# Scaling the message weights and making their low half on GpSimd, with the taps' sums behind the fifth turn

## The chip, the cores and the metric

One core of one Trainium2 chip runs the whole program. The metric is the device time of one execution in microseconds (us), lower is better. The engines are named as in the profile: PE is TensorE's matmul, DVE is VectorE, ACT is ScalarE, POOL is GpSimd, and SP is the engine that issues nearly all transfers.

## The reference

64 graphs of 256 nodes with 256 features go through two layers, each behind a layer norm, a ReLU and a residual sum. The first layer is a graph convolution. The second has a convolution branch (a 1-wide one, conv1, with a batch norm, and then a 17-wide one, conv2, with another), a message branch, and a GRU that joins both.

```python
h = relu(layernorm(x));  x = x + relu(norm_adj @ h @ W.T + b)        # layer 0
h = relu(layernorm(x))                                              # layer 1 on h
c = relu(bn1(conv1(h)));  c = bn2(conv2(c));  x_conv = relu(c + h)
s = h @ w_se.T + b_se;    A = exp(-dist(s, s))
msg = relu(h @ w_msg.T + b_msg);  x_nmp = A @ msg
x = x + gru([x_conv, x_nmp], h)
```

bn1's scale g / sqrt(v + eps) is multiplied into conv1's weights, and bn2's into the 17 taps of conv2.

## The kernel before

The program is written by hand for each engine, with explicit semaphores. An engine executes its own list in order, and a wait_ge holds everything behind it on that engine. There are three stages: the first takes the 64 batches one after the other, the second multiplies spectra, the third runs the GRU. The change touches only the start of the first.

The first stage is a software pipeline of turns. In turn i each engine calls its function first_tensor, first_vector, first_scalar, first_gpsimd or first_sync with i, and each of them does a step for batch i, another for batch i - 1, and so on: statistics of batch i, hd (the normalised input) for i - 1, the aggregation agg (L618) for i - 2, out0 (matmuls with w0, the first matmuls of a turn on PE) for i - 3, the second norm xn for i - 4, transposes (L666) for i - 4, and for i - 5 the products of the second layer. So turn 5 is the first in which batch 0 reaches the second layer: xn is transposed, copied to xt by ACT (L411), split into a high half xxh (ACT, L342) and a low half xxl (DVE, L442), and multiplied on PE with wse (into SXN, 6 matmuls of 256 columns) and then with w1m (into CM1 and CM0, 12 matmuls of 512 columns). In turn 6 DVE adds the bias to CM0 (tcm, L433), and makes uv (L451), which PE's distance product (L627) waits for.

All matmuls of this kind take each operand as a high and a low half, and three products of halves make one product. So each weight has to be split once before its first use: high = copy (ACT), low = weight - high (DVE before the change). For w1m there is a step ahead of that: conv1's half of the raw weights st_w1 is multiplied with the row s1r of bn1's scales (L1388), which ACT copies out of PSUM (L1303, semaphore normrow). w1m has two halves side by side for each input block, conv1's weights and the messages' weights, 128x1024 in all. The change's short description speaks of the messages' weights; the instructions scale columns 0 to 255 of each block, and make the low half of all 1024 columns.

For the taps DVE multiplies bn2's scales into a table and sums it (s2m L1397, s2t L1400, semaphore s2t). The taps themselves are scaled on POOL from turn 10 on.

Before turn 5 ACT, DVE and POOL each wait for clo >= 3 (the low halves of w0, w1m and wse exist) and s2t >= 2 (the taps' sums exist). I call this the barrier. Some buffers of turn 5 and later lie over the staging buffers (st_w1, s2m and their neighbours). PE waits for normrow >= 2 before turn 5 and for clo >= 3 ahead of its first product with wse.

SP's list, with the loads of later batches, hangs on DVE's statistics (semaphores st0 and deg0).

Of the kernel before, what the change touches and what calls it, by code (L numbers as in the profile page):

```python
# [11 lines left out]
ALU = mybir.AluOpType  # L12
# [103 lines left out]
half one ident_in col_in eye2_in w0_in b0_in tt_in w1_in se_in bm_in ft_in gt_in tap0 tap1 s2t  # L116
consts crs diag rows normrow w1s chi clo ones taps
ldx0 ldx1 lda0 lda1 lat0 lat1 st0 ag0a ag0 deg0 degm rs0 dd sd sbias hd ah agg aghi aglo
# [8 lines left out]
def gnn_kernel(nc, x, adj, adjt, w0t, w1mt, wset, wgt, w2r, bc, cols, ftab, gtab, ttab, eye, out):  # L127
# [19 lines left out]
    with ExitStack() as ctx:  # L147
        S = {n: ctx.enter_context(nc.semaphore(n)) for n in NAMES}
# [13 lines left out]
        taps = keep("taps", [119, NW, 256])  # L162
# [88 lines left out]
        TURNS = NB + 11  # L251
# [331 lines left out]
        def first_tensor(e, i):  # L583
# [46 lines left out]
            if live(i, 5):  # L630
                b = i - 5
                e.wait_ge(S["xxhi"], b + 1)
                e.wait_ge(S["xxlo"], b + 1)
                e.wait_ge(S["clo"], 3)
                multiply(e.e, mm3([{c: h[:, c, :] for c in range(2)} for h in wse],
                                  [{c: h[:, c * 256:c * 256 + 256] for c in range(2)} for h in xx],
                                  P[SXN][:, 0:256], True, True, [(0, 0), (1, 1)])).then_inc(S["s"], 1)
# [12 lines left out]
            if live(i, 5):  # L650
                b = i - 5
                for k, n, name, freed in ((CM1, 1, "cm1", "tcm1"), (CM0, 0, "cm0", "tcm0")):
                    e.wait_ge(S[freed], b)
                    multiply(e.e, mm3([{c: h[:, c * 256 + n * 128:c * 256 + n * 128 + 128] for c in range(2)}
                                       for h in xx],
                                      [{c: h[:, c, :] for c in range(2)} for h in w1m],
                                      P[k][:, :], True, True, [(0, 0), (1, 1)])).then_inc(S[name], 1)
# [631 lines left out]
        def _(scalar):  # L1289
# [23 lines left out]

            e.wait_ge(S["clo"], 3)
            e.wait_ge(S["s2t"], 2)
            for i in range(5, TURNS):
                first_scalar(e, i)
# [49 lines left out]
        def _(vector):  # L1367
# [16 lines left out]
            first_vector(e, 3)  # L1384
            e.wait_ge(S["normrow"], 1)
            e.wait_ge(S["w1_in"], 16)
            for k in range(2):
                t = vector.tensor_tensor(st_w1[:, k, 0:256], st_w1[:, k, 0:256], s1r[:, :], ALU.mult)  # L1388
            t.then_inc(S["w1s"], 1)
            first_vector(e, 4)  # L1390
            e.wait_ge(S["chi"], 2)
            vector.tensor_tensor(w1m[1][:, :, :], st_w1[:, :, :], w1m[0][:, :, :], ALU.subtract).then_inc(S["clo"], 1)
            e.wait_ge(S["chi"], 3)
            vector.tensor_tensor(wse[1][:, :, :], st_se[:, :, :], wse[0][:, :, :], ALU.subtract).then_inc(S["clo"], 1)
            e.wait_ge(S["normrow"], 2)
            e.wait_ge(S["tt_in"], 16)
# [3 lines left out]
            vector.tensor_reduce(s2t[:, :], s2m[:, :, :], AX_X, ALU.add).then_inc(S["s2t"], 1)  # L1400
            e.wait_ge(S["clo"], 3)
            e.wait_ge(S["s2t"], 2)
            for i in range(5, TURNS):
                first_vector(e, i)
# [37 lines left out]
        def _(gpsimd):  # L1442
# [13 lines left out]
            gpsimd.tensor_tensor(cold[:, 0:4], cold[:, 20:24], half[:, 0:4], ALU.pow).then_inc(S["crs"], 1)  # L1456
            for i in range(2, 5):
                first_gpsimd(e, i)
            e.wait_ge(S["clo"], 3)
            e.wait_ge(S["s2t"], 2)  # L1460
            for i in range(5, TURNS):
                first_gpsimd(e, i)
# [100 lines left out]
```

## Time and profile before

| what | us |
|---|---|
| median of 3 runs | 1773.26 (1773.23 to 1773.27) |
| the profiled execution's own time | 1773.39 |
| its span (first to last instruction) | 1771.6 |

A row of a timeline has the start in us from the span's beginning, the duration, the engine, the line of the kernel, the operation, its output and inputs, and their shapes.
### The profile page before, as it was taken

What the parts mean: (1) busy time and instruction counts of PE and PEld (TensorE: products, weight loads), DVE (VectorE), ACT (ScalarE), POOL (GpSimd) and SP (SyncE); (2) the same over time, 40 slices, a digit from 0 to 9 for tenths busy, and PEclk for the clock granted to TensorE, in tenths of its full rate; (3) what the DMA queues carried; (4) which work ended last, traced back from release to release, by engine and by line L of the source; (5) the groups of instructions that cost most, each with busy time, mean ns of one, the idle gap of its engine ahead of it and who ended that gap; (6) DMA issues with size and microseconds to landing.
All of it is one profiled execution on the core that took longest, in us unless ns stands there. A gap on an engine that the chain in (4) does not pass through costs nothing.

```text
span 1771.6 us, 30896 instructions
## 1 busy us (share of the span) xinstructions
PE 1757.3 (99%) x10778; PEld 1556.6 (88%) x10778; DVE 1201.1 (68%) x2318; ACT 999.2 (56%) x1787; POOL 817.7 (46%) x988
## 2 busy tenths in 40 slices
PE   8999999999999999999999999999999999999998
PEld 7999999999999999999988888888888888888887
DVE  8999999999999956655664544544545545545445
ACT  6888888888888866666642333332333333333322
POOL 5788888888777637655731221221221212212211
PEclk9999999999999999999999999999999999999999
DMA  6567666666666454444674345445345353454442
GB/s 223 174 201 214 203 211 205 211 204 200 197 192 202 147 167 156 168 166 166 238 213 105 71 105 123 97 107 113 74 112 122 88 119 82 98 120 99 104 96 42
DMA packets 531865, 262.70 MB, mean 148 GB/s; under 512 B 366215, under 2 KB 494471, under 8 KB 531710
## 3 DMA queue, kind: packets, MB, share of 16 engines
q1 hardware_dynamic: 531166, 260.66, 53.5%
q8 instruction: 87, 1.43, 0.4%
q14 instruction: 68, 0.56, 0.1%
q10 hardware_dynamic: 544, 0.07, 0.0%
HBM read 151.58 MB, written 109.05 MB: 147 GB/s over the span
## 4 chain that ended last, share of the span: by engine, by line
PE 96%; issue 1%; DVE 1%; POOL 1%; DMA 1%; ACT 0%; SPq 0%; POOLq 0%; ACTq 0%; DVEq 0%
PE P L111 73%; PE P L618 6%; PE P L1025 4%; PE P L877 4%; PE P L647 4%; PE P L709 4%; PE P L666 2%; PE P L627 1%; DMA at<-in_adjt 0%; POOL axl L581 0%; DMA eye<-in_eye 0%; POOL af L578 0%; DVE sm L489 0%; DVE sm L495 0%; DVE xct L1039 0%
## 5 line engine op out<-in xcount | busy, mean ns | idle before, releaser
L1004 POOL TENSOR_TENSOR xnx1l<-xnf,xnx1h 128x1024 fp32r<-128x1024 f32 x16 | 44.3, 2771 | 393.2 <-ACT xnx1h L997 393.2
L1004 POOL TENSOR_TENSOR xnx0l<-xnf,xnx0h 128x1024 fp32r<-128x1024 f32 x15 | 40.9, 2729 | 272.9 <-ACT xnx0h L997 272.9
L1130 ACT ACTIVATE nn<-gn,col 128x512 f32<-128x512 f32 x64 | 46.4, 725 | 193.4 <-DVE gn L1151 193.4
L1127 ACT ACTIVATE tr<-P,cold 128x512 f32<-128x512 f32 x64 | 44.2, 690 | 179.8 <-PE P L111 179.8
L1147 DVE SCALAR_TENSOR_TENSOR gn<-tr,gn 128x512 f32<-128x512 f32 x64 | 45.2, 706 | 137.3 <-ACT tr L1127 137.3
L578 POOL TENSOR_TENSOR af<-af,at 128x512 f32<-128x512 f32 x64 | 111.9, 1748 | 40.8 <-ACT af L369 39.7
L581 POOL TENSOR_TENSOR axl<-af,axh 128x512 fp32r<-128x512 f32 x64 | 102.8, 1606 | 54.0 <-ACT axh L387 54.0
L618 PE MATMUL P<-ah,hd 128*128 128x256 f32 x512 | 121.9, 381 | 0.0
L1160 DVE SCALAR_TENSOR_TENSOR tz<-tz,tr 128x512 f32<-128x512 f32 x63 | 43.6, 692 | 109.3 <-ACT tz L1141 109.2
L1141 ACT ACTIVATE tz<-P,cold 128x512 f32<-128x512 f32 x63 | 43.4, 689 | 123.2 <-PE P L111 123.2
L111 PE MATMUL P<-w1mh,xxh 128*128 128x512 f32 x256 | 106.5, 416 | 0.0
L618 PEld LDWEIGHTS P<-ah,hd 128*128 128x128 f32 x512 | 93.3, 191 | 10.3
L111 PE MATMUL P<-w1mh,xxl 128*128 128x512 f32 x256 | 100.5, 393 | 0.0
L111 PE MATMUL P<-w1ml,xxh 128*128 128x512 f32 x256 | 100.2, 391 | 0.0
L501 DVE SCALAR_TENSOR_TENSOR x<-x,x 128x512 f32<-128x512 f32 x64 | 99.8, 1559 | 0.1
L902 DVE TENSOR_TENSOR yo<-P,mt 128x512 f32<-128x512 f32 x78 | 53.5, 686 | 65.4 <-PE P L111 65.4
L1151 DVE TENSOR_TENSOR gn<-gn,P 128x512 f32<-128x512 f32 x64 | 44.0, 687 | 65.2 <-PE P L111 64.6
L1039 DVE SCALAR_TENSOR_TENSOR xct<-P,cold,xnf 128x256 f32<-128x256 f32 x128 | 55.7, 477 | 44.9 <-PE P L1025 44.9
L111 PE MATMUL P<-w0h,agh 128*128 128x256 f32 x256 | 76.9, 301 | 4.9 <-DVE w0l L466 2.1
L709 PE MATMUL P<-tt_w,taps 119*128 119x140 f32 (+1 forms) x592 | 80.8, 282 | 0.0
L729 ACT COPY wf<-P 128x420 f32<-128x420 f32 (+1 forms) x94 | 46.8, 512 | 59.5 <-PE P L709 59.3
L1025 PEld LDWEIGHTS P<-gt,yt 64*128 64x128 f32 x1280 | 75.2, 187 | 5.6 <-issue 5.6
(214 smaller groups left out, 6401.3 us busy)
## 6 DMA issues: line engine op xcount, KB each, us to landing
xh_d<-xst SPq DMA_DIRECT2D x64, 320.0 KB, 4.9
y_d<-yo SPq DMA_DIRECT2D x80, 256.0 KB, 2.1
yt<-y_d SPq DMA_DIRECT2D x128, 160.0 KB, 4.5
xl<-xh_d SPq DMA_DIRECT2D x36, 512.0 KB, 4.5
x<-in_x SPq DMA_DIRECT2D x64, 256.0 KB, 2.7
a<-in_adj SPq DMA_DIRECT2D x64, 256.0 KB, 3.0
at<-in_adjt SPq DMA_DIRECT2D x64, 256.0 KB, 4.2
x_d<-x SPq DMA_DIRECT2D x64, 256.0 KB, 4.4
```

The source lines that it names most:

```text
L111: done = e.matmul(o, l, r, start=start, stop=stop, skip_group_check=True)
L501: e.e.scalar_tensor_tensor(out=o[:, :, :], in0=o[:, :, :], scalar=0.0, in1=xs[b % 5][:, :, :], op0=ALU.max, op1=ALU.add).then_inc(S["x2"], 1)
L578: e.e.tensor_tensor(af[:, :], af[:, :], at[b % 7][:, :], ALU.mult).then_inc(S["am"], 1)
L581: e.e.tensor_tensor(ax[1][:, :], af[:, :], ax[0][:, :], ALU.subtract).then_inc(S["axlo"], 1)
L618: t = e.e.matmul(P[AG][:, f * 256:f * 256 + 256], hd[b % 2][:, m, f * 128:f * 128 + 128], ah[b % 2][:, m * 256:m * 256 + 256], start=m == ...
L647: t = e.e.matmul(P[k][:, n * 2 * NT:n * 2 * NT + 2 * NT], h1[b % 2][:, n, c * 128:c * 128 + 128], ft[:, :], start=True, stop=True, skip_gr ...
L709: t = e.e.matmul(P[k][:, m * 140:m * 140 + 140], taps[0:n_rows, j0 + m, c * 128:c * 128 + 128], tt_w[0:n_rows, part * 140:part * 140 + 140 ...
L877: t = e.e.matmul(common(chunk)[:, 0:256], xsum[f % 3][:, c, 128 * chunk:128 * chunk + 128], wsum[f % 3][:, c, :], start=c == 0, stop=c == ...
L902: e.e.tensor_tensor(yo[n % 4][:, :].rearrange("p (q o) -> p q o", q=2), main(chunk)[:, :].rearrange("p (q o) -> p q o", q=2), mt[chunk][:, ...
L1004: e.e.tensor_tensor(o[1][:, :, :], xnf[p % 2][:, :, :, :].rearrange("p c i t -> p c (i t)"), o[0][:, :, :], ALU.subtract).then_inc(done, 1)
L1025: t = e.e.matmul(P[idft_bank(b, o)][:, at + first:at + end], y[rows, q, :], gt[rows, g:g + end - first], start=q == 0, stop=q == 4, skip_g ...
L1039: d = e.e.scalar_tensor_tensor(out=t[:, c, :], in0=P[idft_bank(b, c)][:, at:at + 256], scalar=b2[:, c:c + 1], in1=xnf[p % 2][:, c, n, :], ...
```

## The change

- DVE no longer multiplies st_w1 with s1r (two 128x256) and no longer makes w1m's low half (128x1024). POOL does the first between turns 3 and 4 and the second behind turn 5, and signals the second with a semaphore of its own, wlp. PE waits for wlp ahead of the products with w1m in turn 5.
- DVE makes the taps' sums behind turn 5, not ahead of it.
- The barrier of ACT, DVE and POOL stands behind turn 5, and asks for clo >= 2, since w1m's low half no longer counts there. PE's wait ahead of the wse product is clo >= 2 too.

```diff
--- before.py
+++ after.py
@@ -114,7 +114,7 @@
 
 NAMES = """
 half one ident_in col_in eye2_in w0_in b0_in tt_in w1_in se_in bm_in ft_in gt_in tap0 tap1 s2t
-consts crs diag rows normrow w1s chi clo ones taps
+consts crs diag rows normrow w1s chi clo wlp ones taps
 ldx0 ldx1 lda0 lda1 lat0 lat1 st0 ag0a ag0 deg0 degm rs0 dd sd sbias hd ah agg aghi aglo
 out0 u x2 sx20 sx21 st1 ag1a ag1 rs1 n1b xn xnt xt sxt xxhi xxlo s uvf uvh uv cm0 cm1 tcm0 tcm1 h1 mshi mslo
 dist af am axhi axlo nmp nm snm dft0 dft1 xe0 xe1 sxa0 sxa1 sxb0 sxb1
@@ -631,7 +631,7 @@
                 b = i - 5
                 e.wait_ge(S["xxhi"], b + 1)
                 e.wait_ge(S["xxlo"], b + 1)
-                e.wait_ge(S["clo"], 3)
+                e.wait_ge(S["clo"], 2)
                 multiply(e.e, mm3([{c: h[:, c, :] for c in range(2)} for h in wse],
                                   [{c: h[:, c * 256:c * 256 + 256] for c in range(2)} for h in xx],
                                   P[SXN][:, 0:256], True, True, [(0, 0), (1, 1)])).then_inc(S["s"], 1)
@@ -649,6 +649,7 @@
                     t.then_inc(S[f"dft{c}"], 1)
             if live(i, 5):
                 b = i - 5
+                e.wait_ge(S["wlp"], 1)
                 for k, n, name, freed in ((CM1, 1, "cm1", "tcm1"), (CM0, 0, "cm0", "tcm0")):
                     e.wait_ge(S[freed], b)
                     multiply(e.e, mm3([{c: h[:, c * 256 + n * 128:c * 256 + n * 128 + 128] for c in range(2)}
@@ -1311,9 +1312,10 @@
             scalar.copy(s2r[:, 256:7 * NW], P[CM0][:, 0:7 * NW - 256]).then_inc(S["normrow"], 1)
             first_scalar(e, 4)
 
-            e.wait_ge(S["clo"], 3)
+            first_scalar(e, 5)
+            e.wait_ge(S["clo"], 2)
             e.wait_ge(S["s2t"], 2)
-            for i in range(5, TURNS):
+            for i in range(6, TURNS):
                 first_scalar(e, i)
             for n in range(EARLY, UNITS):
                 if n == UNITS - 6:
@@ -1382,25 +1384,19 @@
             vector.tensor_scalar(cold[:, 8:12], cold[:, 8:12], 0.5, None, ALU.mult)
             vector.tensor_scalar(cold[:, 12:14], col[:, 26:28], 0.5, None, ALU.mult)
             first_vector(e, 3)
-            e.wait_ge(S["normrow"], 1)
-            e.wait_ge(S["w1_in"], 16)
-            for k in range(2):
-                t = vector.tensor_tensor(st_w1[:, k, 0:256], st_w1[:, k, 0:256], s1r[:, :], ALU.mult)
-            t.then_inc(S["w1s"], 1)
             first_vector(e, 4)
-            e.wait_ge(S["chi"], 2)
-            vector.tensor_tensor(w1m[1][:, :, :], st_w1[:, :, :], w1m[0][:, :, :], ALU.subtract).then_inc(S["clo"], 1)
             e.wait_ge(S["chi"], 3)
             vector.tensor_tensor(wse[1][:, :, :], st_se[:, :, :], wse[0][:, :, :], ALU.subtract).then_inc(S["clo"], 1)
+            first_vector(e, 5)
             e.wait_ge(S["normrow"], 2)
             e.wait_ge(S["tt_in"], 16)
             vector.tensor_tensor(s2m[:, :, :], s2r[0:119, :].rearrange("p (j o) -> p j o", o=7),
                                  tt_w[:, 560:567].unsqueeze(1).broadcast_to((119, NW, 7)), ALU.mult).then_inc(S["s2t"], 1)
             e.wait_ge(S["s2t"], 1)
             vector.tensor_reduce(s2t[:, :], s2m[:, :, :], AX_X, ALU.add).then_inc(S["s2t"], 1)
-            e.wait_ge(S["clo"], 3)
+            e.wait_ge(S["clo"], 2)
             e.wait_ge(S["s2t"], 2)
-            for i in range(5, TURNS):
+            for i in range(6, TURNS):
                 first_vector(e, i)
             first_stage_done(e)
             weights_lo(e, 0)
@@ -1454,11 +1450,20 @@
             first_gpsimd(e, 1)
             e.wait_ge(S["consts"], 1)
             gpsimd.tensor_tensor(cold[:, 0:4], cold[:, 20:24], half[:, 0:4], ALU.pow).then_inc(S["crs"], 1)
-            for i in range(2, 5):
+            for i in range(2, 4):
                 first_gpsimd(e, i)
-            e.wait_ge(S["clo"], 3)
+            e.wait_ge(S["normrow"], 1)
+            e.wait_ge(S["w1_in"], 16)
+            for k in range(2):
+                t = gpsimd.tensor_tensor(st_w1[:, k, 0:256], st_w1[:, k, 0:256], s1r[:, :], ALU.mult)
+            t.then_inc(S["w1s"], 1)
+            for i in range(4, 6):
+                first_gpsimd(e, i)
+            e.wait_ge(S["chi"], 2)
+            gpsimd.tensor_tensor(w1m[1][:, :, :], st_w1[:, :, :], w1m[0][:, :, :], ALU.subtract).then_inc(S["wlp"], 1)
+            e.wait_ge(S["clo"], 2)
             e.wait_ge(S["s2t"], 2)
-            for i in range(5, TURNS):
+            for i in range(6, TURNS):
                 first_gpsimd(e, i)
             first_stage_done(e)
             for f in range(NF):
```

How the lists stand now, in the place that counts. On DVE, between turn 4 (it ends with L417) and turn 5 (it begins with L442):

```order
 L417 BN_AGGR sm_90<-sm_90 128x2 x2
 L417 BN_AGGR sm_87<-sm_87 128x2 x2
-L1392 TENSOR_TENSOR w1ml<-st_w_118,w1mh 128x1024
-L1394 TENSOR_TENSOR wsel<-st_se,wseh 128x256
-L1397 TENSOR_TENSOR s2m<-s2r,tt_w 119x259
-L1400 TENSOR_REDUCE s2t<-s2m 119x37
+L1389 TENSOR_TENSOR wsel<-st_se,wseh 128x256
 L442 TENSOR_TENSOR xxl<-P,xxh 128x512
 L461 TENSOR_TENSOR ah_73<-at_111,eye_106 128x512
```

Of four instructions one is left there. On DVE again, between turn 5 (it ends with L535) and turn 6 (it begins with L433):

```order
 L417 BN_AGGR sm_88<-sm_88 128x2 x2
 L535 TENSOR_TENSOR tcm<-P,b1m 128x512
+L1393 TENSOR_TENSOR s2m<-s2r,tt_w 119x259
+L1396 TENSOR_REDUCE s2t<-s2m 119x37
 L433 TENSOR_TENSOR tcm<-P,b1m 128x512
 L442 TENSOR_TENSOR xxl<-P,xxh 128x512
```

The two instructions of the taps' sums came here. On POOL, between turn 5 (it ends with L566 of batch 4, which ACT's hd waits for) and turn 6:

```order
 L564 TENSOR_TENSOR sm_90<-sm_90 128x2
 L566 TENSOR_TENSOR sm_90<-sm_90 128x2
+L1463 TENSOR_TENSOR w1ml<-st_w_118,w1mh 128x1024
 L540 TENSOR_TENSOR sm_88<-guard,sm_88 128x2
 L541 TENSOR_TENSOR sm_88<-guard,sm_88 128x2
```

w1m's low half is made behind all ten small instructions of turn 5.

## Rows read from the trace of the kernel before

**Rows 1.** The page's first part: busy us, share of the span, instructions of each engine.
```profile
PE 1757.3 (99%) x10778; PEld 1556.6 (88%) x10778; DVE 1201.1 (68%) x2318; ACT 999.2 (56%) x1787; POOL 817.7 (46%) x988
```

**Rows 2.** Busy us by window, 100 us of the first stage: stretch, PE, PEld, DVE, ACT, POOL, PEclk, DMA.
```profile
100.00:200.00 100.00, 100.00 (x654) 92.18 (x653) 97.73 (x238) 88.45 (x176) 82.09 (x131) 1.00 0.67 206
```

**Rows 3.** Timeline of PE, turns 3 to 7: start, us, engine, line, operation.
```profile
13.10 0.36 PE L111 MATMUL P<-w0h,agh 128*128 128x256 f32 x1 [2.09 <-DVE w0l L466]
...
21.02 1.89 PE L618 MATMUL P<-ah,hd 128*128 128x256 f32 x8
23.77 0.66 PE L666 MATMUL P<-ident,xn 128*128 128x128 f32 x4 [0.86 <-ACT xn L357]
25.26 0.36 PE L111 MATMUL P<-w0h,agh 128*128 128x256 f32 x1 [0.83 <-DVE agl L423]
...
27.39 2.86 PE L618 MATMUL P<-ah,hd 128*128 128x256 f32 x8
29.99 0.37 PE L111 MATMUL P<-xxh,wseh 128*128 128x256 f32 x1
...
30.79 0.40 PE L111 MATMUL P<-w1mh,xxh 128*128 128x512 f32 x1
...
37.89 0.51 PE L627 MATMUL P<-uv 96*128 96x256 f32 x2 [0.53 <-DVE uv L451]
...
42.52 0.36 PE L111 MATMUL P<-w0h,agh 128*128 128x256 f32 x1 [0.25 <-issue]
```

**Rows 4.** Busy us by window, three single microseconds around the clock's fall.
```profile
23.00:24.00 1.00, 0.23 (x2) 0.23 (x3) 1.00 (x3) 1.00 (x3) 0.92 (x2) 1.00 0.63 172
...
26.00:27.00 1.00, 1.00 (x7) 1.00 (x7) 1.00 (x2) 0.47 (x1) 0.00 (x0) 0.50 1.06 371
...
29.00:30.00 1.00, 1.00 (x6) 0.74 (x4) 0.80 (x2) 0.14 (x2) 0.92 (x3) 0.82 0.94 319
```

**Rows 5.** Timeline of DVE, turns 4 to 6.
```profile
20.29 0.72 DVE L1388 TENSOR_TENSOR st_w<-st_w,s1r 128x256 f32<-128x256 f32 x2
...
25.87 1.19 DVE L1392 TENSOR_TENSOR w1ml<-st_w,w1mh 128x1024 fp32r<-128x1024 f32 x1
...
27.49 0.43 DVE L1397 TENSOR_TENSOR s2m<-s2r,tt_w 119x259 f32<-119x259 f32 x1
...
29.20 0.69 DVE L442 TENSOR_TENSOR xxl<-P,xxh 128x512 fp32r<-128x512 f32 x1 [0.83 <-ACT xxh L342]
...
32.44 0.68 DVE L501 SCALAR_TENSOR_TENSOR x<-x,x 128x512 f32<-128x512 f32 x1
...
36.96 0.88 DVE L451 SCALAR_TENSOR_TENSOR uv<-uvh,col,uvf 96x256 fp32r<-96x256 f32 x2
```

**Rows 6.** Timeline of ACT, turns 5 and 6.
```profile
25.91 0.56 ACT L411 COPY xt<-P 128x512 f32<-128x512 f32 x1
28.45 0.62 ACT L342 CAST xxh<-xt 128x512 fp32r<-128x512 f32 x1 [1.98 <-DVE s2t L1400]
...
34.35 0.59 ACT L411 COPY xt<-P 128x512 f32<-128x512 f32 x1
```

**Rows 7.** Timeline of POOL, turns 4 and 5.
```profile
20.45 0.28 POOL L540 TENSOR_TENSOR sm<-guard,sm 128x2 f32<-128x2 f32 x1 [3.47 <-DVE sm L417]
...
28.51 0.19 POOL L540 TENSOR_TENSOR sm<-guard,sm 128x2 f32<-128x2 f32 x1 [3.64 <-DVE s2t L1400]
...
32.40 0.79 POOL L566 TENSOR_TENSOR sm<-sm 128x2 f32<-128x2 f32 x1
```

**Rows 8.** Timeline of POOL in the second stage, two instructions of 128x1024.
```profile
681.06 2.38 POOL L800 TENSOR_TENSOR xh0l<-xl,xh0h 128x1024 fp32r<-128x1024 f32 x1
...
685.09 3.35 POOL L800 TENSOR_TENSOR xh1l<-xl,xh1h 128x1024 fp32r<-128x1024 f32 x1
```

**Rows 9.** Timeline of DVE at the same place.
```profile
681.37 2.63 DVE L818 SCALAR_TENSOR_TENSOR wsum<-wf 128x512 f32<-128x512 f32 x1
```

**Rows 10.** Line L501 (DVE): duration in ns min/median/max, first and last start.
```profile
L501 DVE SCALAR_TENSOR_TENSOR x<-x,x x64: 676/1666/1675, 18.0 to 625.2; 128x512 f32<-128x512 f32 x64
```

## The prediction, made before the result was known

> **What bounds the kernel now.** I read the page's first part, then the windows by stretch, then the timelines of the four engines between 20 and 43 us. PE is busy for 1757.3 us of a span of 1771.6 [rows 1], and in the middle of the first stage for 100.00 of 100 us, with DVE at 97.73 [rows 2]. So PE sets the time, and a change to the start can only move the moment from which PE is never idle. That moment is turn 7: its first matmul starts at 42.52, and the last real wait before it is at 37.89, where the distance product stood 0.53 us for DVE's uv [rows 3]. I therefore forecast one number: by how much the distance product of turn 6, and with it 42.52, moves. The rest of the span follows rigidly.
>
> How that start is made now. The barrier opens when the taps' sums are done: ACT and POOL go on at 28.45 and 28.51 [rows 6, 7]. ACT's xxh then takes 0.62, DVE's xxl runs from 29.20 to 29.89 [rows 5], and PE's wse product starts at 29.99 [rows 3]. PE shows no idle time ahead of it, but only because its clock had fallen: it is 0.50 in the microsecond at 26 and 0.82 in the one at 29 [rows 4], so it was back at about 29.4. The aggregation at 27.39 took 2.86 us, where the one at 21.02 took 1.89 [rows 3]. By the remaining work PE would have been ready at about 29.7. So the barrier costs PE only 0.3 us now.
>
> **Part 1, scaling st_w1 on POOL.** The pair leaves DVE at 20.29 and frees 0.64 us there (0.72 less the overlap) [rows 5]. But the next step but one on DVE reads out0 of batch 1, which PE finishes as it goes over to the aggregation at 21.02 [rows 3], read out at about 21.25 against 21.5 now: 0.3 us is kept. POOL is idle for 3.47 us before 20.45 [rows 7], so its pair is hidden. Its price: a POOL instruction of 1024 columns takes 2.38 [rows 8], so 256 columns about 0.6 to 0.75, the pair 1.5, from 18.7 to 20.2, just ahead of what POOL does next. If it ran 0.5 longer it would hold the second norm of batch 0 by that and take the 0.3 back.
>
> **Part 2, the barrier behind turn 5.** DVE finishes turn 4's statistics at 25.95 now (w1m's low half starts at 25.87) and at 25.65 then. ACT's xxh of batch 0 needs only xt, which ends at 26.47 now [rows 6] and 0.2 earlier then, and runs to 26.9; DVE's xxl runs from 26.95 instead of 29.20. So DVE's turn 5 starts 2.25 us earlier: w1m's low half (1.1) and the taps' sums (0.9, from 27.49 to the barrier) [rows 5] are out of its way, and it idles about as long for xxh as now. PE does not gain as much. Its out0 comes at 25.0, the aggregation still runs largely at the low clock, and the wse product goes from about 29.3 to 30.05, 0.75 earlier than now (30.79 is when the w1m product starts [rows 3]).
>
> **Part 3, w1m's low half on POOL, behind turn 5.** This is the term that decides. POOL's turn 5 starts when DVE's statistics come, 25.75, no longer at 28.51. It took from 28.51 to 33.19, 4.68 us; of that 0.6 was the last instruction's, 0.79 long where such a one takes 0.20, under DVE's L501 (32.44 to 33.12) [rows 5, 7]. So 4.1 us is the price, and it ends at 29.85. (Bounds: 3.6 with no overlap with DVE at all, 4.7 as in the row: 29.35 to 30.45.) Then the 128x1024 instruction. The nearest row is 2.38, the largest 3.35 [rows 8]; I take 2.38, since the 3.35 one began under a DVE instruction with two SBUF inputs and DVE's L461 will be over. It ends at 32.23. PE, ready at 30.05, waits for wlp until 32.33: **a new wait of 2.3 us**, and the w1m product starts 1.54 later than at 30.79. Behind it in PE's queue stand 12 matmuls, the transposes of batch 1 and all of turn 6.
>
> On DVE, L501 of turn 5 comes 3.24 us behind xxl (29.20 to 32.44 [rows 5]), at 30.19, when POOL's long instruction has run for 0.34. The nearest case: DVE's L818 came 0.31 after POOL's L800, took 2.63 us and ended 0.56 after it [rows 8, 9]; and L501 itself is 0.68 alone but 1.67 in the median, where POOL works beside it [rows 10]. So L501 ends at 32.8, against 33.12 now. **The 2.25 us that DVE had won are down to 0.3.** Then the taps' sums cost 0.9, and DVE's turn 6 starts 0.6 later than now, at 35.9.
>
> What is late next is ACT's xt of batch 1. It waits for the transposes behind the w1m product: 32.33 + 2.8 + 0.6 gives 35.75 against 34.35 [rows 6], and xxh, right behind it, runs from 36.37 to 36.99. The barrier, open at 35.9, is no limit there; POOL's turn 6 starts with it, about 1 us later than now and in step with the rest. DVE's xxl of batch 1 waits for xxh until 37.06, and uv, 1.05 behind xxl by the present list, starts at 38.1 against 36.96 [rows 5]. So the distance product is 1.15 later too: 37.89 becomes 39.05. SP's loads hang on DVE's statistics ahead of L501, which come early, and cost nothing.
>
> One rule of the Trainium skill speaks against this place. SBUF — State Buffer, "Who interferes with whom", says that "a DVE instruction with two SBUF inputs contends with a GpSimd instruction that reads SBUF", and that whoever comes first keeps the other out for its whole length. Rows 8 and 9 agree (DVE's ended 0.56 after POOL's), so by the rule too L501 ends at 32.8 and the sum stays; but it makes the order of arrival, 0.34 us apart, a case of its own (rival 3).
>
> **Part 4, the clock.** The fall at 26 came after two short gaps of 0.86 and 0.83 us with only transposes between them [rows 3] (PE busy 0.23 of the microsecond at 23 [rows 4]). The new wait is 2.3 us in one piece, with nothing in it. A gap of 2.09 us, up to 13.10 [rows 3], went without a fall, though, so both ends are open: 0, or a fall of the same length, 3.4 us at half speed (from just before 26 to 29.36, by rows 4), which takes 1.7 us of PE's time. It would strike the w1m product and the transposes, and those lead straight to xt and uv, so all of it counts. I take the fall, as the new wait is emptier than the stretch before the old one.
>
> **Sum.** 1.15 + 1.7 = +2.85 us. Against the profiled execution (1773.39, 1.8 us more than its span) that is 1776.2, and against the median of 1773.26, which I use, **1776.1**, 0.16% more.
>
> **Rivals.**
> 1. *No fall of the clock.* Everything else as above: +1.15, **1774.4**. For it: the gap of 2.09 us without one [rows 3].
> 2. *The low half comes in time.* If POOL's small instructions and the long one together took no more than PE needs, PE would start the w1m product at 30.05, DVE's L501 would be free early, and 0.75 us of gain would stay: **1772.5**. It needs POOL to start the long instruction by 27.7, 1.6 us under my lowest bound; only a much faster small chain would do. Little speaks for it.
> 3. *L501 comes first* (the slower side). If POOL's small chain ends later than 30.19, 0.34 us after my estimate, DVE takes the lock, and the long instruction starts at 30.87 and ends at 33.25. DVE keeps its gain, but it can't use it: the w1m product starts 1 us later still, so +2.15, with the fall +3.85, **1777.1**. For it: a margin of 0.34 against a spread of 1.1 in the chain. Against: most of the spread in the row was L501's own lock.
> 4. *The collision stays.* DVE has 2.3 us of slack in 100 [rows 2], 0.2 a turn. If the shift left one more meeting of POOL and DVE per turn, of 1.0 us (1.67 less 0.68 [rows 10]), some 57 turns would cost 0.8 each: about **1819**. Against: from turn 7 on the lists are those of before, PE leads, and the present pattern comes out of a start that was as irregular.
>
> **How the numbers follow.** Forecast 0.44; rival 1 0.26; rival 2 0.08; rival 3 0.17; rival 4 0.03; 0.02 for what I don't see. A measurement of this kernel can tell 0.2% (3.5 us) from no change, so "same" is 1769.7 to 1776.8. Rival 1, most of 2 and most of the forecast lie in it, rival 3 in part: same 0.77, slower 0.20, faster 0.03. The sum's terms are known to half a microsecond each. The range leaves out rival 2 and rival 4 and takes in rival 3: 1773.2 to 1777.5.
>
> **What would show it.** In the profile of the changed kernel: PE idle for about 2.3 us ahead of L111 with w1m, released by POOL's L1463; L1463 of 2.4 us from 29.9; DVE's L501 in turn 5 about 2.6 us long; L342 of batch 0 at 26.3; granted clock at 0.50 from about 33 to 36; the last wait before PE is full at L627, near 40. The forecast is wrong if L1463 ends before 30, if L501 is 0.68 long there, or if PE has no wait on wlp.

## The result, and the profile after

The changed kernel takes 1776.59 us in the median of 17 runs (1774.38 to 1778.65), the kernel before 1773.27 (17 runs): ratio 1.0017, 95% interval 1.001 to 1.0024. That is 3.3 us more, just under the 0.2% (3.5 us) that the prediction took as what can be told from no change; the forecast was 1776.1. (Three single executions among all runs, two of the kernel before and one of e1, took 1950 us and more at a mean granted clock of 0.85 and less, and are in no comparison.)

The runs of the changed kernel are not spread evenly. Sorted they form three groups: five at 1774.4 to 1774.9, eight at 1776.1 to 1777.0, four at 1778.0 to 1778.7. Those of the kernel before lie within about 1 us, but for one.

The record also has the mean granted clock of each run, to 0.001. A low stretch as long as the one in [rows 4] takes 1.7 us of some 1772, so 0.001, and the profiled executions agree: 1.000 in e3 and e11 below, with none in the first 45 us; 0.999 in the kernel before, with one; 0.998 in the changed kernel, with two. Each profile shows one more at the very end of the program, which lowers the mean by up to 0.001. So a run at 1.000 had none ahead of the end, one at 0.998 at least one, and one at 0.997 at least two. No run of the changed kernel is at 1.000, and the number of stretches does not sort its groups: four of the five lowest runs and all four of the upper group are at 0.998, and the five at 0.997 are all in the middle group. So it is their place that counts.

The profiled execution of the changed kernel is one of the upper group, 1778.06 with a span of 1776.3. Against [rows 1] PE is busy for 1.5 us more, with as many matmuls; the span is 4.7 us longer, so 3.2 us are idle time of PE. The 1.5 fit one more stretch of low clock, shown below. The first part of the page of the changed kernel (engine, busy us, share of the span, instructions):

```profile
PE 1758.8 (99%) x10778; PEld 1556.9 (88%) x10778; DVE 1200.7 (68%) x2315; ACT 999.9 (56%) x1787; POOL 820.4 (46%) x991
```

The timeline of PE in the changed kernel, turns 4 to 7 (start, us, engine, line, operation; the w1m product's wait is new, and the other line numbers are a little higher than before):

```profile
25.40 0.66 PE L667 MATMUL P<-ident,xn 128*128 128x128 f32 x4 [2.26 <-ACT xn L357]
26.97 0.36 PE L111 MATMUL P<-w0h,agh 128*128 128x256 f32 x1 [0.92 <-DVE agl L423]
...
28.45 1.89 PE L618 MATMUL P<-ah,hd 128*128 128x256 f32 x8
...
34.04 0.50 PE L111 MATMUL P<-w1mh,xxh 128*128 128x512 f32 x1 [3.00 <-POOL w1ml L1463]
...
42.52 0.51 PE L627 MATMUL P<-uv 96*128 96x256 f32 x2 [0.27 <-DVE uv L451]
...
47.14 0.36 PE L111 MATMUL P<-w0h,agh 128*128 128x256 f32 x1 [0.21 <-issue]
```

Against [rows 3]: a new row with a wait stands there, 3.00 us for POOL's L1463, and the w1m product starts at 34.04 instead of 30.79. The distance product moved from 37.89 to 42.52, by 4.63, and the time of the profiled execution by 4.67. The transposes already wait 2.26 us for xn at 25.40, where they waited 0.86.

The granted clock in the same execution, first from the windows of PE alone (stretch, length, PE busy, PEclk, DMA share, GB/s):

```profile
14.00:16.00 2.00, 2.00 (x11) 0.61 1.06 343
16.00:18.00 2.00, 2.00 (x7) 0.54 0.81 265
```

And around the new wait, from the windows of all engines (stretch, length, then busy us of PE, PEld, DVE, ACT and POOL, PEclk, DMA share, GB/s):

```profile
35.00:36.00 1.00, 1.00 (x4) 0.79 (x3) 1.00 (x5) 0.00 (x0) 0.00 (x0) 0.50 0.35 27
37.00:38.00 1.00, 1.00 (x4) 0.81 (x3) 0.76 (x3) 0.00 (x0) 0.07 (x1) 0.50 0.86 244
38.00:39.00 1.00, 1.00 (x7) 0.81 (x7) 0.13 (x1) 0.00 (x0) 0.92 (x3) 0.83 0.66 166
```

There are two stretches of low clock, one from about 14.4 to 17.9 and one from about 35.0 to 38.4, each about as long as the one in [rows 4]. The second follows the new wait and lies over the w1m product. The first is not a part of the forecast: it lies ahead of turn 4, behind a gap of 2.1 us that the kernel before has too. PE's waits in the changed kernel up to 760 us (what waits, what ends it: total us, count, largest):

```profile
PE P L111 <- POOL w1ml L1463: 3.0, 1, 3.0
PE P L667 <- ACT xn L357: 2.3, 1, 2.3
PE P L111 <- DVE w0l L466: 2.1, 1, 2.1
```

The timeline of DVE, the same execution:

```profile
28.71 0.69 DVE L442 TENSOR_TENSOR xxl<-P,xxh 128x512 fp32r<-128x512 f32 x1 [0.93 <-ACT xxh L342]
...
31.95 2.59 DVE L501 SCALAR_TENSOR_TENSOR x<-x,x 128x512 f32<-128x512 f32 x1
...
38.87 0.69 DVE L433 TENSOR_TENSOR tcm<-P,b1m 128x512 f32<-128x512 f32 x1 [1.07 <-PE P L111]
40.53 0.69 DVE L442 TENSOR_TENSOR xxl<-P,xxh 128x512 fp32r<-128x512 f32 x1 [0.97 <-ACT xxh L342]
```

And of POOL:

```profile
20.53 1.92 POOL L1458 TENSOR_TENSOR st_w<-st_w,s1r 128x256 f32<-128x256 f32 x2 [2.86 <-ACT b1m L1305]
...
31.65 2.34 POOL L1463 TENSOR_TENSOR w1ml<-st_w,w1mh 128x1024 fp32r<-128x1024 f32 x1
37.93 0.20 POOL L540 TENSOR_TENSOR sm<-guard,sm 128x2 f32<-128x2 f32 x1 [3.94 <-DVE s2t L1396]
```

POOL's long instruction takes 2.34 us; DVE's L501 comes 0.30 behind its start, takes 2.59 and ends 0.55 after it, as [rows 8, 9] had it (2.63 and 0.56). But DVE then waits 1.07 us for PE (L433) and 0.97 for ACT's xxh: L501's hold is real, and off the path. POOL's pair (L1458) starts as soon as ACT has copied s1r and b1m (the signal comes behind the second), and takes 1.92.

### The profile page after: what moved, and what is told of

Read it like the earlier page. It is cut to its first block, busy times and chain, and to the rows that moved or that the text cites. A ratio compares the mean times of both kernels' runs of the same rounds, so it can differ in the third digit from the quotient of the medians.

```text
span 1776.3 us, 30896 instructions
## 1 busy us (share of the span) xinstructions
PE 1758.8 (99%) x10778; PEld 1556.9 (88%) x10778; DVE 1200.7 (68%) x2315; ACT 999.9 (56%) x1787; POOL 820.4 (46%) x991
## 4 chain that ended last, share of the span: by engine, by line
PE 96%; POOL 1%; issue 1%; ACT 1%; DVE 1%; DMA 0%; POOLq 0%; ACTq 0%; DVEq 0%
PE P L111 72%; PE P L618 6%; PE P L1026 4%; PE P L878 4%; PE P L647 4%; PE P L710 4%; PE P L667 2%; PE P L627 1%; POOL axl L581 0%; POOL af L578 0%; DMA x<-in_x 0%; POOL sm L560 0%; POOL w1ml L1463 0%; POOL sm L550 0%; ACT hd L403 0%
## 5 line engine op out<-in xcount | busy, mean ns | idle before, releaser
L501 DVE SCALAR_TENSOR_TENSOR x<-x,x 128x512 f32<-128x512 f32 x64 | 101.6, 1588 | 0.1
```

The lines of the kernel that those rows point to most:

```text
L501: e.e.scalar_tensor_tensor(out=o[:, :, :], in0=o[:, :, :], scalar=0.0, in1=xs[b % 5][:, :, :], op0=ALU.max, op1=ALU.add).then_inc(S["x2"], 1)
```

## The experiments

Each kernel below was run with the kernel before on the same chip. The kernel before gave medians of 1773.26, 1773.19 and 1773.19 in the three sets; all differences are against those. Theory A is the forecast's: PE's wait for the low half, and the fall of the clock behind it. B: POOL's pair is the loss. C: the barrier behind turn 5 is the loss. D, formed from the profile above: the fall ahead of turn 4 comes through because POOL's pair follows s1r at once.

**e1, w1m's low half back on DVE**, behind its turn 4 and ahead of wsel.

```diff
+            e.wait_ge(S["chi"], 2)
+            vector.tensor_tensor(w1m[1][:, :, :], st_w1[:, :, :], w1m[0][:, :, :], ALU.subtract).then_inc(S["wlp"], 1)
-            gpsimd.tensor_tensor(w1m[1][:, :, :], st_w1[:, :, :], w1m[0][:, :, :], ALU.subtract).then_inc(S["wlp"], 1)
```

> The changed kernel, but w1m's low half is made by DVE ahead of turn 5, as before the change. Theory A (the wait for the low half, and the clock's fall behind it, are the loss): the w1m product of turn 5 starts at about 30, L501 is 0.68 us long, no wait on the low half, and the time is 1.0 us under the kernel before, 1772.2. Rival B (the scaling pair on POOL, 1.92 us, holds batch 0's norm): 1775 or more, since the pair stays on POOL. Rival C (the barrier and the taps' sums behind turn 5 hold ACT and POOL in turn 6): 1775 or more, since they stay.

Measured: 1774.66 (1773.37 to 1775.95, 11 runs), ratio 1.0007 (0.9998 to 1.0015), with groups near 1773.5, 1774.7 and 1775.9. About 2 us of the 3.3 are gone, but not all, and the gain of 1 us that A promised did not come. In the profiled execution (1774.85) PE has no wait for the low half and L501 takes 0.68, as A said; but the w1m product starts at 32.51, not at 30. The timeline of PE in e1:

```profile
25.44 0.66 PE L667 MATMUL P<-ident,xn 128*128 128x128 f32 x4 [1.88 <-ACT xn L357]
...
32.51 0.40 PE L111 MATMUL P<-w1mh,xxh 128*128 128x512 f32 x1
```

PE waits longer for xn than the 0.86 of [rows 3], and the clock is low twice, from about 13.6 to 17 and from 27.3 to 30.7. How much of e1's median each of these holds is not separated.

**e2, the low half on POOL, but ahead of turn 5.**

```diff
-            for i in range(4, 6):
-                first_gpsimd(e, i)
+            first_gpsimd(e, 4)
             e.wait_ge(S["chi"], 2)
             gpsimd.tensor_tensor(w1m[1][:, :, :], st_w1[:, :, :], w1m[0][:, :, :], ALU.subtract).then_inc(S["wlp"], 1)
+            first_gpsimd(e, 5)
```

> The changed kernel, but POOL makes w1m's low half between turns 4 and 5, not behind turn 5. Theory A: it is done by about 27 to 28.5, PE does not wait for it, DVE's wsel (two SBUF inputs) is held by about 1 us in place of L501 by 2; 1772.3, range 1771.8 to 1773.5. Rival B or C: 1775 or more, since the pair and the barrier stay. Were GpSimd's 2.35 us itself the loss, wherever it stands, the time would stay at 1776.

Measured: 1773.83 (1773.4 to 1775.6, 11 runs), ratio 1.0005 (0.9996 to 1.0013); 0.3 above the expected range. The timeline of POOL in e2:

```profile
21.03 1.92 POOL L1458 TENSOR_TENSOR st_w<-st_w,s1r 128x256 f32<-128x256 f32 x2 [2.77 <-ACT b1m L1305]
...
26.92 2.39 POOL L1462 TENSOR_TENSOR w1ml<-st_w,w1mh 128x1024 fp32r<-128x1024 f32 x1
```

And of DVE in e2:

```profile
27.94 1.64 DVE L1389 TENSOR_TENSOR wsel<-st_se,wseh 128x256 fp32r<-128x256 f32 x1
```

The instruction is as long as ever (2.39), it now holds DVE's wsel to 1.64 us, and PE does not wait for it. So 2.8 us of the loss hang on its place in POOL's list. B and C as the whole cause are out, since the pair and the barrier stayed. The profiled execution (1775.18) has two low stretches at the places of e1's.

**e4, the low half made twice**, PE waiting for the second.

```diff
-            gpsimd.tensor_tensor(w1m[1][:, :, :], st_w1[:, :, :], w1m[0][:, :, :], ALU.subtract).then_inc(S["wlp"], 1)
+            for k in range(2):
+                e.wait_ge(S["wlp"], k)
+                gpsimd.tensor_tensor(w1m[1][:, :, :], st_w1[:, :, :], w1m[0][:, :, :], ALU.subtract).then_inc(S["wlp"], 1)
-                e.wait_ge(S["wlp"], 1)
+                e.wait_ge(S["wlp"], 2)
```

> The changed kernel, but POOL makes w1m's low half twice, one behind the other, and PE waits for the second. Theory A: the wait on PE grows by one instruction, 2.4 us, and the time by as much: 1779.0. Rivals B and C: the low half is not what is late, so less than 0.5 us more.

Measured: 1779.23 (1778.72 to 1781.95, 5 runs), ratio 1.0037 (1.0025 to 1.0049). The pair of instructions took 5.12 us and the wait of PE 3.95, by the timelines of POOL and then of PE in e4:

```profile
30.02 5.12 POOL L1465 TENSOR_TENSOR w1ml<-st_w,w1mh 128x1024 fp32r<-128x1024 f32 x2
```

The same wait on PE:

```profile
35.19 0.50 PE L111 MATMUL P<-w1mh,xxh 128*128 128x512 f32 x1 [3.95 <-POOL w1ml L1465]
```

2.6 us more than the changed kernel for 2.8 us more work on POOL: nothing covers the low half. The wait itself is only 0.95 longer than the changed kernel's 3.00, for an expected 2.4, since this execution has no fall ahead of turn 4: POOL began at 30.02, where it had begun at 31.65.

**e3 and e8, filler matmuls.** e3 has 12 ahead of the wait for the low half, e8 these and 11 more ahead of the first product with w0.

```diff
+                if b == 0:
+                    for n in range(12):
+                        e.e.matmul(P[CM1][:, 0:128], ident[:, :], ident[:, :], start=True, stop=True, skip_group_check=True)
                 e.wait_ge(S["wlp"], 1)
```

> The changed kernel, with 12 float32 matmuls of 128x128 (identity times identity, into the bank that the w1m product overwrites) ahead of PE's wait for the low half, some 2.2 us of work in a wait of 2.3 to 3. Theory A with its clock part: the granted clock stays at 1.00 behind the wait, the time falls by about 1.7 to 1774.7, and the runs spread less than those of the changed kernel (1774.4 to 1778.7). If the clock's fall costs nothing on the path: 1776.5, spread as before.

> The changed kernel with both sets of filler matmuls, ahead of the first product with w0 and ahead of the wait for the low half. Theories A and D: no fall of the clock on the path is left, only the wait for the low half: 1774.6, most runs within 0.7 us of it, so of the 3.3 us that the change costs half is the clock's. If the clock is not the cause of the spread: median 1776 or more, spread as with the change.

Measured: e3 1776.21 (1774.38 to 1777.87, 11 runs), ratio 1.0018 (1.0009 to 1.0026); e8 1775.37 (1774.78 to 1776.23), ratio 1.0013 (1.0004 to 1.0022). Both medians missed what A expected. e8's profile says why, first PE, then POOL:

```profile
31.23 2.84 PE L658 MATMUL P<-ident 128*128 128x128 f32 x24
33.83 0.48 PE L111 MATMUL P<-w1mh,xxh 128*128 128x512 f32 x1
```

The low half in the same execution:

```profile
30.14 2.37 POOL L1471 TENSOR_TENSOR w1ml<-st_w,w1mh 128x1024 fp32r<-128x1024 f32 x1
```

The clock was low from about 26 to 29.5, ahead of the fillers (12 matmuls, 24 records). They ran at full clock, 2.84 us as in e3, but began late, and the w1m product started 1.3 us after the low half was there. e11's expectation below has this wrong, with the clock "low when they ran". Twelve were too many, and the medians of e3 and e8 as tests of the clock are blurred by that. By the mean clocks on record they say more. e3's one run at 1.000 took 1774.4, its five at 0.999 took 1775.1 to 1776.2, and its five at 0.998 took 1776.7 to 1777.9: the more low clock, the longer, without an overlap. The four runs of e8 at 1.000 took 1774.8 to 1775.4. e3's profiled execution, on the other hand, has the wait and no low clock at all from 8 to 45 us, and it took 1774.38. The timeline of POOL in e3:

```profile
18.59 1.41 POOL L1462 TENSOR_TENSOR st_w<-st_w,s1r 128x256 f32<-128x256 f32 x2 [1.73 <-ACT b1m L1309]
...
29.56 2.35 POOL L1467 TENSOR_TENSOR w1ml<-st_w,w1mh 128x1024 fp32r<-128x1024 f32 x1
```

The distance product on PE in e3:

```profile
38.85 0.51 PE L627 MATMUL P<-uv 96*128 96x256 f32 x2 [0.28 <-DVE uv L451]
```

And the clock in e3 (windows of PE, columns as above):

```profile
12.00:18.00 6.00, 4.72 (x32) 1.00 0.97 335
...
31.00:40.00 9.00, 8.26 (x50) 1.00 0.46 147
```

**e7, only the early fillers; e11, the early ones and 7 ahead of the wait.** The early ones stand in PE's list ahead of the first product with w0, as in e8.

```diff
+                if b == 0:
+                    for n in range(11):
+                        e.e.matmul(P[CM1][:, 0:128], ones[:, :], ones[:, :], start=True, stop=True, skip_group_check=True)
                 e.wait_ge(S["aghi"], b + 1)
```

> The changed kernel, with 11 float32 matmuls of 128x128 (ones times ones, into a free bank) ahead of PE's first product with w0, where it stood 2.1 us for DVE. Theory D: the clock no longer falls ahead of turn 4, so the group near 1778 goes: nearly all runs between 1774.4 and 1776.9, median 1776.3. If that fall has no part in the spread, runs near 1778 stay, one in four.

> The changed kernel with the filler matmuls ahead of the first w0 product, and only 7 (not 12) ahead of the wait for the low half: 12 overran the wait by 1.2 us in the profile where the clock was low when they ran. If the clock's fall behind the wait is what parts the groups at 1774.9 and 1776.7: all runs within 0.5 us of 1774.9. If not, both groups stay.

Measured: e7 1774.94 (1774.76 to 1776.97, 11 runs), ratio 1.0012 (1.0003 to 1.0021): seven runs at 1774.8 to 1775.0, four at 1776.5 to 1777.0, none near 1778. e11 1774.82 (1774.42 to 1775.27, 11 runs), ratio 1.0009 (1.0 to 1.0018): one group only. The clock in e7 (windows of PE):

```profile
12.00:18.00 6.00, 6.00 (x48) 1.00 0.92 303
...
31.00:40.00 9.00, 7.51 (x34) 0.81 0.48 140
```

The same windows of e11:

```profile
12.00:18.00 6.00, 6.00 (x47) 1.00 0.95 321
...
31.00:40.00 9.00, 7.52 (x44) 1.00 0.49 147
```

And PE's wait and its distance product in e11:

```profile
32.27 0.50 PE L111 MATMUL P<-w1mh,xxh 128*128 128x512 f32 x1 [1.19 <-POOL w1ml L1471]
...
39.17 0.50 PE L631 MATMUL P<-uv 96*128 96x256 f32 x2 [0.29 <-DVE uv L451]
```

This is the test of the clock's part. e7's profiled execution (1776.53) has low clock behind the wait, 0.81 over 9 us, which is 3.4 us at half speed; e11's (1774.71) has none. With the early gap filled the upper group goes (no run of e7, e8 and e11 is above 1777.0, 33 in all, against four of 17), and with the wait filled in part the middle group goes too: no run of e11 is above 1775.3, against 12 of 17 of the changed kernel. From e7 to e11 alone it is 4 of 11 against none of 11, which is few. Nor do the fillers end all low clock: four of e11's runs (1774.73 to 1774.94) have a mean of 0.998, so at least one low stretch, which cost nothing that shows. Where it lay is not on record; ahead of the wait, as e12's second below, would do.

What is left, 1.6 us over the kernel before, is not on the clock's account: it is the wait, with what the pair and the barrier cost in this kernel, and 0.1 of it is the early fillers' own (the first w0 product starts 0.94 behind DVE's w0l in e11, and 0.83 without them).

**e5 and e6, the parts alone.** e5 puts POOL's pair back on DVE, between its turns 3 and 4; e6 puts both weight steps back, and leaves only the taps' sums and the barrier behind turn 5.

```diff
-            for k in range(2):
-                t = gpsimd.tensor_tensor(st_w1[:, k, 0:256], st_w1[:, k, 0:256], s1r[:, :], ALU.mult)
+            for k in range(2):
+                t = vector.tensor_tensor(st_w1[:, k, 0:256], st_w1[:, k, 0:256], s1r[:, :], ALU.mult)
```

> The changed kernel, but DVE multiplies st_w1 with s1r between turns 3 and 4, as before the change; GpSimd still makes the low half behind turn 5. The changed kernel's times lie in groups near 1774.8, 1776.5 and 1778.1. Theory D: a fall of the clock ahead of turn 4 delays s1r by 1.7 us, which the kernel before absorbed (DVE reached the pair 1.7 us after s1r was there), while GpSimd's pair starts the moment that s1r is there. So here the group near 1778 goes and the median is 1776.0, the wait for the low half staying. Theory A alone, with no part for the pair: median 1776.6 and the same spread. Rival B (the pair is the whole loss): 1773.5.

> Both weight steps on DVE as before the change; only the taps' sums and the barrier stand behind turn 5. Theories A and D: no loss is left and the barrier's 0.3 to 1 us is gained, with the narrow spread of the kernel before: 1772.5, range 1772.0 to 1773.3. Rival C (the barrier's new place holds ACT and POOL): 1774 or more.

Measured: e5 1776.58 (1774.37 to 1777.98, 11 runs), ratio 1.0017 (1.0008 to 1.0026): the same median as the changed kernel, so the pair is worth nothing in it; two runs stayed at 1778, which D did not expect; their mean clock is 0.997, so each had at least two low stretches. e6 1773.95 (1772.84 to 1774.88, 11 runs), ratio 1.0002 (0.9993 to 1.0011). The gain I expected is missing, and its profile (1774.33) shows where it went. The timeline of POOL in e6:

```profile
34.69 0.20 POOL L540 TENSOR_TENSOR sm<-guard,sm 128x2 f32<-128x2 f32 x1 [3.13 <-DVE s2t L1403]
...
39.87 1.37 POOL L566 TENSOR_TENSOR sm<-sm 128x2 f32<-128x2 f32 x1
...
43.22 1.27 POOL L581 TENSOR_TENSOR axl<-af,axh 128x512 fp32r<-128x512 f32 x1 [0.73 <-ACT axh L387]
```

And of PE in e6:

```profile
37.27 0.50 PE L627 MATMUL P<-uv 96*128 96x256 f32 x2 [1.29 <-DVE uv L451]
...
44.63 0.36 PE L111 MATMUL P<-axh,msh 128*128 128x256 f32 x1 [1.09 <-POOL axl L581]
```

The distance product came at 37.27, 0.62 us earlier than before. But POOL stood 3.13 us for the taps' sums, its small instructions of turn 6 then ran beside DVE's locks (L566 1.37 us long instead of 0.20), af and axl were late, and PE waited 1.09 us for axl in turn 7. So C is true as a mechanism in this kernel: with the taps' sums and the barrier behind turn 5, POOL gives back what DVE wins.

**e9 and e10, the barrier without that.** e9 is the kernel before, with nothing changed but the place of the waits, behind turn 5 on ACT, DVE and POOL. e10 is e6 with POOL's wait moved into turn 6, ahead of the product with af.

The edit of e9, on ACT; DVE and POOL have the same:

```diff
+            first_scalar(e, 5)
             e.wait_ge(S["clo"], 3)
             e.wait_ge(S["s2t"], 2)
-            for i in range(5, TURNS):
+            for i in range(6, TURNS):
```

The edit of e10, in first_gpsimd:

```diff
+                e.wait_ge(S["clo"], 2)
+                e.wait_ge(S["s2t"], 2)
                 e.wait_ge(S["af"], b + 1)
```

> The kernel before, with nothing moved on DVE or GpSimd, only the waits of ACT, DVE and GpSimd for clo and s2t put behind turn 5. DVE's xxl of batch 0 follows the taps' sums at 28.4 (29.20 before), and the barrier is open long before turn 6, so nobody is held there: 0.8 us under the kernel before, 1772.4. If the barrier's place is worth nothing: 1773.2.

> The kernel with only the barrier and the taps' sums behind turn 5 (median 1773.95), but GpSimd waits for them inside turn 6, ahead of its product with af, so that its ten small instructions of turn 6 run before DVE's sums. Theory C (behind turn 5 the barrier holds GpSimd's turn 6, whose small instructions then run under DVE's locks, and PE waits 1.1 us for axl in turn 7): that wait is gone and the time is 1772.3, 1 us under the kernel before. Otherwise 1773.2 to 1774, and PE still waits for axl in turn 7.

Measured: e9 1772.79 (1772.18 to 1773.27, 11 runs), ratio 0.9998 (0.9989 to 1.0007); e10 1772.51 (1772.03 to 1773.21, 11 runs), ratio 0.9997 (0.9988 to 1.0006). Both medians lie under the kernel before's 1773.19, by 0.4 and 0.7 us, and both intervals hold 1. In the trace e10 does what was expected: the waits of PE for axl add up to 0.8 us in the first stage, as before, where e6 had 1.8; and the distance product stands at 36.90. e10's profiled execution is also one without any low clock from 8 to 45 us, where e6's had the early fall, so part of the difference between the two profiles is that; the medians differ by 1.4. The clock is not the cause of that: e6's four runs at a mean of 1.000 took 1773.7 to 1774.1, e10's four took 1772.0 to 1772.5. Four runs of e6 at 0.999 took 1772.8 to 1773.0, though, so a low stretch can also shift POOL out of DVE's way, and the loss doesn't come in every execution. The group of PE's waits for axl up to 760 us, first in e10 (what waits, what ends it: total us, count, largest):

```profile
PE P L111 <- POOL axl L583: 0.8, 2, 0.5
```

The same group in e6:

```profile
PE P L111 <- POOL axl L581: 1.8, 3, 1.1
```

**e12, the changed kernel again**, for another profile.

> The changed kernel once more, for a profile of another execution. The time follows from the stretches of low clock on the path: 1774.7 with none between 12 and 45 us (or with one that PE's wait for the low half hides), 1776.5 with one behind that wait, 1778.1 with one more ahead of turn 4.

Measured: 1777.02, one run. The clock in e12 (windows of PE):

```profile
14.00:16.00 2.00, 2.00 (x10) 0.50 0.79 260
...
28.00:30.00 2.00, 2.00 (x10) 0.50 0.72 254
...
34.00:36.00 2.00, 1.46 (x6) 1.00 0.00 0
```

And the timeline of PE in e12:

```profile
34.54 0.50 PE L111 MATMUL P<-w1mh,xxh 128*128 128x512 f32 x1 [1.56 <-POOL w1ml L1463]
...
41.43 0.50 PE L627 MATMUL P<-uv 96*128 96x256 f32 x2 [0.30 <-DVE uv L451]
```

The early fall is there, the second one lies at 28 to 31, ahead of the wait, which it only shortens (1.56 us), and none comes behind it. My three classes gave 1776.5 for a fall behind the wait and 1778.1 for both; this mix I had not listed. It comes out 2.3 us over e11's profiled execution, which has neither fall; 0.6 of that is a later start (see the table), and the 1.65 that stay are one low stretch.

**The forecast's one number, over all profiles.** I said that only the start of the distance product of turn 6 counts, 37.89 before, in an execution of 1773.39 (the last two columns are explained below the table):

| kernel | distance product | moved | time of that execution, moved | w0l starts | moved from w0l |
|---|---|---|---|---|---|
| changed | 42.52 | +4.63 | +4.67 | 12.44 | +4.46 |
| e12, changed again | 41.43 | +3.54 | +3.63 | 13.04 | +2.77 |
| e4, low half twice | 43.65 | +5.76 | +5.83 | 12.63 | +5.40 |
| e7, early fillers | 40.97 | +3.08 | +3.14 | 12.70 | +2.65 |
| e5, pair on DVE | 40.77 | +2.88 | +2.85 | 12.62 | +2.53 |
| e1, low half on DVE | 39.26 | +1.37 | +1.46 | 12.85 | +0.79 |
| e2, low half early | 39.62 | +1.73 | +1.79 | 13.03 | +0.97 |
| e8, 23 fillers | 40.67 | +2.78 | +2.84 | 12.74 | +2.31 |
| e11, fillers | 39.17 | +1.28 | +1.32 | 12.43 | +1.12 |
| e3, fillers | 38.85 | +0.96 | +0.99 | 12.15 | +1.08 |
| e9, waits only | 37.61 | -0.28 | -0.18 | 12.41 | -0.42 |
| e10 | 36.90 | -0.99 | -0.88 | 12.68 | -1.40 |
| e6, barrier only | 37.27 | -0.62 | +0.94 | 12.47 | -0.82 |

All but e6 agree within 0.11 us; e6 lost 1.6 later, partly at axl.

The last two columns take out that executions don't start alike. DVE's low half of w0 (L466), which the first product with w0 waits for, starts between 12.15 and 13.04 in them. In the kernel before:

```profile
12.27 0.68 DVE L466 TENSOR_TENSOR w0l<-st_w,w0h 128x512 fp32r<-128x512 f32 x1
```

Counted from there (25.62 us in the kernel before) the parts add up. The changed kernel without low clock on the path is at +1.08 and +1.12 (e3, e11, which are that but for the fillers). One low stretch on the path adds 1.4 to 1.7 to that (e5, e7, e12), two add 3.4 (the changed kernel), and the overrun of e8's fillers adds 1.2.

## Why the prediction was right, point by point

- *A rigid shift behind turn 7.* Right, by the table.
- *The low half is late, and PE waits for it.* Right, and the term that decides. The instruction took 2.34 (2.38 said), and with no low clock before it (e3, e5, e7, e11) POOL's small chain ended where said: it started at 29.56 to 30.09 (29.85 said). The w1m product of e11 starts at 32.27 (32.33 said).
- *L501 is held.* Right in size (2.59 against 2.63), and of no weight. I had called the loss of DVE's lead a part of the chain and then followed xt, which was the right branch. The Trainium skill's SBUF — State Buffer, "Who interferes with whom", has this lock, and e2 shows the same on wsel.
- *Its sum without the clock, +1.15.* Right within 0.1, counted from w0l: +1.08 in e3, +1.12 in e11. POOL's pair takes 1.41 in e3 (1.5 said) and 1.86 to 1.92 in the other profiles that have it on POOL, where DVE's L461 falls among its two instructions. I had that in Part 1 as "if it ran 0.5 longer", with the norm of batch 0 held, and that doesn't show: the low half starts 17.3 to 17.4 us behind w0l in all six executions without the early fall, with the short pair (e3), the long one (e4, e7, e8, e11), and the pair on DVE (e5). By the medians e11 is 1.6 above the kernel before, and the 0.5 beyond the path of its profile is not explained.
- *The clock falls behind the wait and costs 1.7.* Right in mechanism and size: the groups lie 1.7 apart, and e7 against e11 shows both. But I took it as the usual case, and it is not shown to be that: with the early gap filled only 4 of e7's 11 runs lie in the group that has it. The other seven, and five of the 17 of the changed kernel, lie near rival 1's 1774.4.
- *What was missing: a fall ahead of turn 4.* [Rows 3] show a gap of 2.09 us up to 13.10, and I used it as evidence that such a gap goes without a fall. In the profile of the changed kernel the same gap has one. TensorE: Matmul & The Clock Gate in the Trainium skill, "What's actually happening", says that the gate's own time does not start with the kernel; the traces agree as far as the first low stretch comes at about 14.4 in the changed kernel's first profile and at 26 in the kernel before's, behind nearly the same start. That the phase of that time is the reason is my guess, and no run shows it. e7, with the early gap filled, has no upper group. With the gap left open the median is the middle group for two reasons, a fall behind the wait (e5 and e7) or one ahead of turn 4 (e12), and the forecast had only the first. That the median came within 0.5 us of 1776.1 is in part luck: it is the middle one of three groups, and some of its runs are there by a fall that the forecast said would not come.
- *The barrier costs 0.3, and POOL's turn 6 stays "in step with the rest".* True of the changed kernel, where af waits for ACT (POOL idle behind its chain), and wrong in e6, where PE waits 1.8 us in all for axl. It doesn't follow from the low half being off the path alone: e1 and e2 have PE's waits for axl as before, 0.8 and 0.7.

What stays open in part: why the kernel before spreads so little. Low clock does come in it. Of its 87 runs beside the experiments 37 have a mean of 1.000 (median 1773.14), 34 one of 0.999 (1773.17) and 16 one of 0.998 (1773.57), so by the medians the low stretches cost it 0.4 us at most. In its profile the stretch lies at 26 to 29.4, ahead of the wse product, which has to wait for DVE's xxl until 29.99 in any case. For an early fall there is no profile of it. e6, with both steps on DVE, has one and reads 0.6 later at the distance product than e10, counted from w0l, not 1.7. That fits a DVE that reaches the pair late anyway (20.55 in e6, against 20.29 in [rows 5]), but e5, with the pair alone on DVE, still has two runs near 1778, and no profile of those. So D is likely where both steps are on DVE, and not shown as the rule.

## What to carry to other kernels

Work moved to an idle engine is not free when that engine's list is a chain of small dependent steps: its start is the end of the chain, so try it ahead of the chain, where its consumer is furthest (e2 took 2.8 us off the median by that alone). Follow a moved barrier to every engine that stands behind it one turn later, since a gain on one can be given back on another (e6). And where PE is the bound, a wait of 2 to 3 us of PE can cost more than its length (1.4 to 1.7 us more here), so look at all runs, not at the median. Groups a fixed distance apart point to the clock, and a few filler matmuls test it, if they don't overrun the wait. What sorts the groups is where the low stretches lie, not how many there are. And before two profiles are set against each other, take out their different starts: 0.9 us here, as much as a term of the sum.

## What the runs showed of the hardware

- The same program, run again, meets the low clock at other places: in the executions profiled here low stretches began at about 14, 26, 28, 34 or 35 us, or there was none up to 45 us (e3, e10, e11). Each was about 3.4 us long at half speed, which is 1.7 us of PE's work. On the path it moved the distance product by 1.4 to 1.7 us (e5, e7, e12); e6's early one by 0.6; e12's second, ahead of a wait, by nothing that shows.
- The gap of 2.1 us on PE ahead of the first w0 product was followed by low clock at about 14 us in five profiled executions (changed, e1, e2, e6, e12) and by none there in five (before, e3, e4, e5, e10; nor in e9, with 2.3 us); with 11 small matmuls in it none of three (e7, e8, e11) has low clock there.
- A GpSimd tensor_tensor with float32 inputs in SBUF took 0.7 us for 128x256 (two in 1.41) and 2.34 to 2.39 for 128x1024. Where a DVE instruction with two SBUF inputs (L461) fell among the pair, the pair took 1.86 to 1.92. DVE's L501 (128x512, 0.68 alone), come 0.30 behind GpSimd's 128x1024, ended 0.55 us after it (changed, e3); wsel (128x256, 0.39 alone) in e2 ended 0.27 after it.
